# A coupled-oscillator scan: stage values of q moved from SBUF to PSUM, and their squares from VectorE to ScalarE

## The reference

```
i_couple = tanh(q) @ coupling.T
dq = q - q**3 / 3 - p + drive + i_couple + bias
dp = 0.08 * (q + 0.7 - 0.8 * p)
q2 = q + 0.5*DT*dq1;  q3 = q + 0.5*DT*dq2;  q4 = q + DT*dq3
q_next = clip(q + DT/6 * (dq1 + 2*dq2 + 2*dq3 + dq4), -20, 20)     (p likewise)
```

## Time and profile before

| what | value |
|---|---|
| time, median of 3 runs | 1496.73 us (1496.61 to 1496.75) |
| profiled execution, span from its first to its last instruction | 1494.5 us |
| median less that span (what lies around it) | 2.2 us |
| TensorE busy in matmuls, in weight loads | 1429.7 us (96%), 1399.6 us (94%) |
| VectorE busy | 1443.0 us (97%), 11274 instructions |
| ScalarE busy | 724.5 us (48%), 4839 instructions |
| granted clock of TensorE | 0.999 of full speed |
| time that all DMA packets took | 7.6% of 16 engines' span |

### The profile page before, as it was taken

One profiled execution on the slowest core, in us unless ns is written; L12 is line 12 of the kernel. 1 busy time (PEld: TensorE's weight loads), 2 busy tenths in 40 slices (PEclk: granted clock), 3 DMA queues, 4 the chain that ended last, 5 costly groups with the idle time before them and its releaser, 6 DMA issues.

```text
span 1494.5 us, 90834 instructions
## 1 busy us (share of the span) xinstructions
PE 1429.7 (96%) x37025; PEld 1399.6 (94%) x37025; DVE 1443.0 (97%) x11274; ACT 724.5 (48%) x4839; POOL 21.3 (1%) x45
## 2 busy tenths in 40 slices
PE   2578999999999999999999999999999999999998
PEld 0467999999999999999999999999999999999998
DVE  7999999999999999999999999999999999999991
ACT  3344455455455545545554544555455455544541
POOL 0100000000000000000000000000000000000000
PEclk9999999999999999999999999999999999999999
DMA  9200000000000000000000000000000000000000
GB/s 228 46 7 14 8 4 8 21 8 4 25 4 22 7 19 11 4 25 4 22 7 13 16 4 25 4 21 8 11 18 4 25 4 21 8 8 22 4 22 22
DMA packets 11942, 28.41 MB, mean 19 GB/s; under 512 B 1537, under 2 KB 5889, under 8 KB 11393
## 3 DMA queue, kind: packets, MB, share of 16 engines
q1 hardware_dynamic: 11520, 22.57, 6.0%
q10 hardware_dynamic: 2, 0.03, 0.0%
HBM read 18.40 MB, written 4.19 MB: 15 GB/s over the span
## 4 chain that ended last, share of the span: by engine, by line
PE 90%; DVE 6%; ACT 0%; issue 0%; POOLq 0%; DVEq 0%; POOL 0%; ACTq 0%
PE scan_ps L559 52%; PE gu_ps L310 23%; PE y_ps L322 15%; DVE th L631 1%; DVE q_stage L669 1%; DVE with_q L625 1%; DVE q_sq L635 1%; DVE scan_ps L643 1%; DVE q_stage L667 1%; DVE q_cub L638 0%; DVE p_part L625 0%; DVE with_p L625 0%; DVE q_raw L669 0%; DVE q_raw L667 0%; DVE p_state L747 0%; DVE hist L654 0%
## 5 line engine op out<-in xcount | busy, mean ns | idle before, releaser
L559 PE MATMUL scan_ps<-th,wscan 128*128 128x32 f16 (+1 forms) x32768 | 1006.0, 175 | 24.7 <-ACT th L597 24.5
L559 PEld LDWEIGHTS scan_ps<-th,wscan 128*128 128x128 f16 x32768 | 924.5, 96 | 42.1 <-ACT th L597 33.2
L597 ACT ACTIVATE th<-q_stage 128x16 f16<-128x16 f32 x1536 | 318.7, 208 | 524.5 <-DVE q_stage L667 524.5
L310 PE MATMUL gu_ps<-hist,wffn 128*128 128x128 f32 x2816 | 503.8, 285 | 0.0
L310 PEld LDWEIGHTS gu_ps<-hist,wffn 128*128 128x128 f32 x2816 | 394.4, 192 | 0.0
L631 DVE TENSOR_TENSOR th<-t,th 128x16 f16<-128x16 f32 x2048 | 358.1, 175 | 0.3
L322 PE MATMUL y_ps<-wffn,h 128*128 128x128 f32 x1408 | 323.7, 313 | 0.0
L599 ACT ACTIVATE t<-q_stage 128x16 f32<-128x16 f32 x1536 | 306.2, 199 | 0.0
L322 PEld LDWEIGHTS y_ps<-wffn,h 128*128 128x128 f32 x1408 | 209.7, 189 | 0.4 <-DVE h L338 0.4
L597 ACT ACTIVATE th<-q_raw 128x16 f16<-128x16 f32 x512 | 106.3, 208 | 184.7 <-DVE q_raw L667 174.8
L388 ACT ACTIVATE sum_r<-dr,constant 128x64 f32<-128x64 f32 x528 | 174.2, 333 | 16.9 <-DMA dr<-drive 16.9
(11 more groups left out here) (41 smaller groups left out, 562.8 us busy)
## 6 DMA issues: line engine op xcount, KB each, us to landing
raw<-packed SPq DMA_DIRECT2D x11, 768.0 KB, 10.4
dr<-drive SPq DMA_DIRECT2D x34, 128.0 KB, 3.0
xres<-x SPq DMA_DIRECT2D x16, 256.0 KB, 3.6
out<-osb SPq DMA_DIRECT2D x16, 256.0 KB, 3.0
coup<-coupling_t SPq DMA_DIRECT2D x1, 1024.0 KB, 12.5
sc<-scales ACTq DMA_DIRECT2D x1, 33.0 KB
q_raw<-cond_t SPq DMA_DIRECT2D x1, 16.0 KB, 5.5
bias<-bias_t SPq DMA_DIRECT2D x1, 2.0 KB, 6.2
```

The costliest lines, as they stand in the source:

```text
L310: i = nc.tensor.matmul(gu_ps[b][:, half * P:(half + 1) * P], wffn[:, u, j * P:(j + 1) * P], hist[1 - f.parity][:, kt].rearrange("p t b -> ...
L559: i = nc.tensor.matmul(to if both else to[:, 0], wscan[:, w, part, kt, cols], moving if both else moving[:, 0], start=first, stop=last, sk ...
L597: nc.scalar.activation(th[s % 2][:, c, 0, :], q[:, c, :], ACT.Tanh, scale=1.0 / S).then_inc(now.tanh_hi, 1)
```

## The change

q2, q3 and q4 (`q_stage`) no longer lie in SBUF. They lie in PSUM, in the banks in which the local part lies: `scan_ps` grows from 3 banks to 4, the first half of q in the second bank and the second half in the third. The reduces of stages 0 to 2 write there, ScalarE's tanh reads there. `q_raw` (the input of stage 0) stays in SBUF.

In stages 1 to 3 of each step (a step's stages 2 to 4, in the words of the reference) q squared is made by ScalarE, in one instruction of 32 numbers behind the four tanhs, and signalled by a new semaphore `squared`. `cube` waits for it. VectorE's own square is left in stage 0 alone. All of VectorE's instructions that read `q_stage` now stand behind that wait: `cube`, the `with_q2`/`with_q3` rows and the `p_part` sums. The sign of the square changes, and with it two operations.

```diff
-CUBE = [-COEF[STAGE_COEF[i]] / (3 * S * S) for i in range(4)]
+CUBE = [COEF[STAGE_COEF[i]] / (3 * S * S) for i in range(4)]
...
-LOCALS = STEPS * 22
+LOCALS = STEPS * 19
...
+        self.squared = sem("squared")
...
-        q_stage = [sb(f"q_stage{i}", [P, KT, B]) for i in (2, 3, 4)]
...
-        scan_ps = ctx.enter_context(nc.psum_tensor("scan_ps", [P, 6 * APART], F32))
+        scan_ps = ctx.enter_context(nc.psum_tensor("scan_ps", [P, 8 * APART], F32))
...
-            slots = scan_ps[:, half * 3 * APART:(half + 1) * 3 * APART].rearrange("p (k r) -> p k r", k=3)
+            slots = scan_ps[:, half * 5 * APART:(half * 5 + 3) * APART].rearrange("p (k r) -> p k r", k=3)
...
-        local_ps = scan_ps[:, 2 * APART:4 * APART].rearrange("p (h r) -> p h r", h=2)[:, :, 0:HB]
+        middle = scan_ps[:, 2 * APART:8 * APART].rearrange("p (h r) -> p h r", h=2)
+        local_ps = middle[:, :, 0:HB]
+        q_stage = [middle[:, :, (4 + i) * HB:(5 + i) * HB] for i in range(3)]
...
+        def q_half(i, half):
+
+            if i == 0:
+                return q_raw[:, half * HC:(half + 1) * HC, :]
+            return q_stage[i - 1][:, half].rearrange("p (c b) -> p c b", b=B)
...
-                    nc.scalar.activation(t32[:, c, :], q[:, c, :], ACT.Tanh,
+                    nc.scalar.activation(t32[:, c, :], q, ACT.Tanh,
                                          scale=1.0 / S).then_inc(now.tanh_32, 1)
+                if s % 4:
+                    nc.scalar.activation(halves(q_sq[:, :, :]), q_stage[s % 4 - 1], ACT.Square,
+                                         scale=CUBE[s % 4] ** 0.5).then_inc(now.squared, 1)
...
+            def cube(s):
+
+                i = s % 4
+                dve.wait_ge(now.squared, s - s // 4)
+                return local(nc.vector.scalar_tensor_tensor(halves(q_cub[:, :, :]), halves(q_sq[:, :, :]), OWN[i],
+                                                            q_stage[i - 1], ALU.subtract, ALU.mult))
...
+            def add_staged(to, row, column, base):
+
+                q = q_stage[column - BY_Q2]
+                return add(halves(to[:, :, :]), q, float(BY[row, column]), halves(base[:, :, :]))
+
+            def add_p_staged(i):
+
+                return add(halves(p_part[i][:, :, :]), halves(p_part[i - 1][:, :, :]), P_SUM[i], q_stage[i - 1])
...
-                nc.vector.tensor_reduce(q_next[:, 0:HC, :], three[0], AX.X, ALU.add).then_inc(now.q_ready, 1)
+                nc.vector.tensor_reduce(q_half(following, 0), three[0], AX.X, ALU.add).then_inc(now.q_ready, 1)
...
                 s = 4 * t + 1
                 ffn_part(s)
-                dve.wait_ge(now.q_ready, 2 * s)
-                squared = square(1, q2)
                 low_part(s, 0)
-                dve.wait_ge(now.local, squared)
-                cubed = cube(1, q2)
                 low_part(s, 1)
+                add(p_part[0][:, :, :], p_state[:, :, :], P_SUM[0], q1)
+                cubed = cube(s)
+                row3 = add_p(t, 3, 1)
                 dve.wait_ge(now.local, cubed)
                 local_in(s)
-                add(p_part[0][:, :, :], p_state[:, :, :], P_SUM[0], q1)
-                add_q(with_q2[0], 2, BY_Q2, q2, with_q1[1][:, :, :])
-                row3 = add_p(t, 3, 1)
+                add_staged(with_q2[0], 2, BY_Q2, with_q1[1])
                 finish(s)
...
```

More of the change, by code:

```diff
@@ L588, in act_block @@
             for s in range(STAGES):
-                q = q_raw if s % 4 == 0 else q_stage[s % 4 - 1]
                 for half in range(2):
                     c = slice(half * HC, (half + 1) * HC)
+                    q = q_half(s % 4, half)
                     if s:
@@ L596, in act_block @@
                         act.wait_ge(before.q_ready, 2 * STAGES - 1 + half)
[L597 removed]
+                    nc.scalar.activation(th[s % 2][:, c, 0, :], q, ACT.Tanh,
                                          scale=1.0 / S).then_inc(now.tanh_hi, 1)
[L599 removed]
+                    nc.scalar.activation(t32[:, c, :], q, ACT.Tanh,
                                          scale=1.0 / S).then_inc(now.tanh_32, 1)
+                if s % 4:
+                    nc.scalar.activation(halves(q_sq[:, :, :]), q_stage[s % 4 - 1], ACT.Square,
+                                         scale=CUBE[s % 4] ** 0.5).then_inc(now.squared, 1)
                 if s == 1 and before:
@@ L632, in low_part, with square_first, cube_first @@
                                         ALU.subtract).then_inc(now.tanh_lo, 1)
[L634 to L639, removed]
+            def square_first(q):
+                return local(nc.vector.scalar_tensor_tensor(q_sq[:, :, :], q, CUBE[0], q, ALU.mult, ALU.mult))
+            def cube_first(q):
+                return local(nc.vector.scalar_tensor_tensor(q_cub[:, :, :], q_sq[:, :, :], OWN[0], q,
+                                                            ALU.subtract, ALU.mult))
+            def cube(s):
[3 more added lines that the diff above has]
+                                                            q_stage[i - 1], ALU.subtract, ALU.mult))
             def local_in(s):
@@ L643, in local_in @@
                 nc.vector.scalar_tensor_tensor(local_ps, halves(linear[i]), UNIT[i], halves(q_cub[:, :, :]),
-                                               ALU.mult, ALU.add).then_inc(now.first_half, 1)
+                                               ALU.mult, ALU.subtract).then_inc(now.first_half, 1)
             def add_p(step, first, rows):
@@ L663, in finish @@
                 i = s % 4
-                q_next = q_raw if i == 3 else q_stage[i]
+                following = (i + 1) % 4
                 dve.wait_ge(now.first_half, 2 * s + 2)
-                nc.vector.tensor_reduce(q_next[:, 0:HC, :], three[0], AX.X, ALU.add).then_inc(now.q_ready, 1)
+                nc.vector.tensor_reduce(q_half(following, 0), three[0], AX.X, ALU.add).then_inc(now.q_ready, 1)
                 dve.wait_ge(now.second_half, s + 1)
-                nc.vector.tensor_reduce(q_next[:, HC:KT, :], three[1], AX.X, ALU.add).then_inc(now.q_ready, 1)
+                nc.vector.tensor_reduce(q_half(following, 1), three[1], AX.X, ALU.add).then_inc(now.q_ready, 1)
             for t in range(STEPS):
                 q1 = hist[now.parity][:, :, t - 1, :] if t else hist[1 - now.parity][:, :, STEPS - 1, :]
-                q2, q3, q4 = (x[:, :, :] for x in q_stage)
                 s = 4 * t
@@ L693, in dve_block @@
                     dve.wait_ge(before.clipped, STEPS)
-                squared = square(0, q1)
+                squared = square_first(q1)
                 low_part(s, 1)
                 dve.wait_ge(now.local, squared)
-                cubed = cube(0, q1)
+                cubed = cube_first(q1)
                 add_q(with_q1[0], 1, BY_Q1, q1, with_p[:, 1])
@@ L721, in dve_block @@
                 add_q(with_q1[2], 3, BY_Q1, q1, with_p[:, 3])
-                dve.wait_ge(now.q_ready, 2 * s)
-                squared = square(2, q3)
                 low_part(s, 0)
-                dve.wait_ge(now.local, squared)
-                cubed = cube(2, q3)
                 low_part(s, 1)
+                cubed = cube(s)
+                p2 = add_p_staged(1)
                 dve.wait_ge(now.local, cubed)
                 local_in(s)
-                p2 = add(p_part[1][:, :, :], p_part[0][:, :, :], P_SUM[1], q2)
-                with_23 = add_q(with_q2[1], 3, BY_Q2, q2, with_q1[2][:, :, :])
+                with_23 = add_staged(with_q2[1], 3, BY_Q2, with_q1[2])
                 dve.wait_ge(now.local, p2)
-                add(p_part[2][:, :, :], p_part[1][:, :, :], P_SUM[2], q3)
+                add_p_staged(2)
+                dve.wait_ge(now.local, with_23)
+                add_staged(with_q3, 3, BY_Q3, with_q2[1])
                 finish(s)
                 s = 4 * t + 3
[L737 to L740, removed]
                 low_part(s, 0)
-                p4 = add(p_part[3][:, :, :], p_part[2][:, :, :], P_SUM[3], q4)
                 low_part(s, 1)
-                dve.wait_ge(now.local, squared)
-                cubed = cube(3, q4)
+                cubed = cube(s)
+                p4 = add_p_staged(3)
+                dve.wait_ge(now.local, cubed)
+                local_in(s)
                 dve.wait_ge(now.local, p4)
@@ L749, in dve_block @@
                                                        ALU.max, ALU.min))
-                dve.wait_ge(now.local, cubed)
-                local_in(s)
                 if t + 1 == HS:
```

## The result

The changed kernel takes 1539.5 us (1538.8 to 1540.5) against 1496.7 us: a ratio of 1.0288 (95% interval 1.0275 to 1.0301). It is slower by 42.8 us where 39.3 were forecast.

The account below looks back on a forecast made before the run. Bound: the wait ending last in each stage's loop, not busy shares. 240 steps x 0.17 = 41 us, plus 1 for block 0, less 3 for output pieces, gave +39: 1536 us, 2.6% slower; range 1508 to 1613 with 0.80.

Parts of the forecast that it names:

- What bounds the kernel: Each stage is a loop of reduce, tanh, products, reduce; TensorE, VectorE and the local part meet within some 0.03 us.
- Stage by stage: Stages 0 to 3 of a step: 1.37, 1.35, 1.43, 1.43 us, a step 0.17 longer than before.
- The cube's start: VectorE's cube in stages 2 and 3 starts 0.77 us after the first reduce, where it stood at 0.68.
- The square as a close second: ScalarE's square lasts 0.18 us and is there at R + 0.58, just ahead of the cube at R + 0.60.
- The rule of 0.22: A VectorE instruction reading the result of the one just before starts 0.22 us after it; an independent one 0.10 to 0.12.
- VectorE's access to PSUM: Writing q to PSUM makes a reduce 0.22 us and tanh start 0.25 after it; reading q there adds nothing.
- Rival 2: VectorE's reads of q in PSUM cost 0.06 us more each: +0.30 a step beyond the forecast, 1613 us; chance 0.06.
- The sum: Whole kernel: 240 steps x 0.17 = 41 us, block 0 adds 1, output pieces take off 3: +39, 1536 us.
- The term for the output pieces: Stages 1 with an output piece: VectorE's idle time swallows most of it, some 30 at 0.1, 3 us off; least certain.
- TensorE waiting for tanh hundreds of times: Sign that the forecast is right: TensorE's listed waits for tanh rise to hundreds, where there were 65.
- Block 0 and the others about equally long: Sign that the forecast is right: block 0, without FFN, lasts about as long as the blocks with it.
- Rival 1: ScalarE's tanhs gain nothing from PSUM, so the cube waits for the square: +0.63 us a step, 1655 us; chance 0.07.

Follow-up runs that it names:

- the third experiment: Changed kernel with VectorE reordered: first with_p row made at the next step's start, p_part sums and with_q2 row moved forward; 1482.7 us, ratio 0.9901 to the kernel before.
- the fourth experiment: Changed kernel with q_stage back in SBUF, square still on ScalarE and VectorE's order kept; 1631.8 us, ratio 1.0897 to the kernel before.

## Why the prediction was right, point by point

- *What bounds the kernel*: a stage as a loop, with three bounds within 0.03 us. Right: the step grew with the two reduces that came later, and with TensorE back at the bound in the third experiment the step is 5.36, 4 x 1.34.
- *Stage by stage*: 1.37, 1.35, 1.43, 1.43 forecast, 1.36, 1.36, 1.44, 1.43 measured: 0.17 a step was the term, and it held.
- *The cube's start*: 0.77 forecast, 0.79 and 0.78 measured, but by errors that cancel, which was luck. A tanh from PSUM lasts 0.18, not 0.16, and stands 0.06 to 0.08 behind the one before, not 0.06; the second reduce comes 0.15 after the first ahead of stage 2 and, where TensorE no longer holds it, 0.12 ahead of stage 3 (611.80 and 611.92), not 0.17. The groups by shape:

```profile
L605 ACT ACTIVATE th<-scan_ps 128x16 f16<-128x16 f32 x1536 | 266.8, 185 | 558.2 <-DVE scan_ps L694 558.2
L607 ACT ACTIVATE t<-scan_ps 128x16 f32<-128x16 f32 x1536 | 262.2, 182 | 0.0
...
L610 ACT ACTIVATE q_sq<-scan_ps 128x32 f32<-128x32 f32 x768 | 162.8, 212 | 0.0
```

- *The square as a close second*: closer than forecast, a tie. It lasts 212 ns on average, not 180.
- *The rule of 0.22 for an instruction that reads VectorE's own last result*: the two rows that it was read from have an independent one between them (at 594.30). It held: 0.22 with one between (611.48 to 611.70), 0.21 with none (p_state to with_p, 612.91 to 613.12).
- *VectorE's access to PSUM*: the write costs less than was put in, the read nothing. The reduce before, then the reduce and the cube after:

```profile
L667 DVE TENSOR_REDUCE q_stage<-scan_ps 128x16 f32<-128x48 f32 x768 | 158.8, 207 | 4.7 <-PE scan_ps L559 1.0
```

```profile
L694 DVE TENSOR_REDUCE scan_ps<-scan_ps 128x16 f32<-128x48 f32 x768 | 163.2, 213 | 7.6 <-PE scan_ps L567 0.7
...
L656 DVE SCALAR_TENSOR_TENSOR q_cub<-q_sq,scan_ps 128x32 f32<-128x32 f32 x768 | 140.4, 183 | 0.0
```

  The reduce lasts 213 ns, with 207 when it wrote to SBUF and 0.22 us forecast; the cube with q from PSUM 183, as much as its like from SBUF, and its room is 0.10 (611.15 to 611.25), as it was (595.43 to 595.53). Rival 2, with 0.06 more for each read, is out. This is also where the Trainium skill ("Perfetto Trace Analysis", section "Optimizing Scalar/DVE Operations") and this trace differ: 125 ns for VectorE on PSUM against 60 on SBUF would have shown as some 65 ns for each read.
- *The sum*: the main term, 0.17 x 240 = 41 us, held. Block 0 lost 2.4 us, not 1 (87.9 to 90.3 from reduce to reduce): its stages 1 and 2 last 1.40 and 1.45, not 1.35 and 1.43. The term for the output pieces, -3 us, held too: a stage 1 with one went from 1.46 to 1.36, and there are two in a block. What the sum left out goes the other way. After the four stages 1 of a block with a third FFN product the second reduce waits for TensorE (it comes 0.20 after the first, not 0.15), and stage 2 lasts 1.49 instead of 1.44. Where `with_p` waits for `sum_r`, twice a block, stage 3 lasts 1.49, 0.07 over the others, where that wait added 0.04 before. Together that is, over the 15 blocks with the FFN, 15 x (4 x 0.05 + 2 x 0.03) = 4 us. 41 + 2.4 - 3 + 4 is 44, about what the two profiled executions differ by (1538.7 against 1494.5 us); the medians differ by 42.8, since the profiled execution of the changed kernel was its slowest (1540.5).
- *The signs*: "TensorE waiting for tanh hundreds of times" was wrong as a sign. The waiting is there, in stages 3 and 0 as forecast, and only the weight loads show it. "Block 0 and the others about equally long" held: 90.3 us from reduce to reduce in block 0, 90.4 in block 6.
- *Rival 1* (ScalarE gains nothing from PSUM, 1655 us) was worked out for a kernel much like the one of the fourth experiment: 1631.8, with stages of 1.36, 1.46, 1.59 and 1.57 where the rival had 1.37, 1.47, 1.60 and 1.60. In the changed kernel the tanhs last 0.18 and stand 0.06 to 0.08 apart, so it is out.

## What to carry to other kernels

Work that is taken off a busy engine is worth only what it took from the path: here 61 us of VectorE's time went, and the kernel lost 43, since the result came back later, and two waits of VectorE for results of its own stood between it and the reduce, one behind the other. When an input comes later, write anew what stands behind it: put beside its wait what doesn't need it, put two dependent rows two places apart, and move behind the hand-over what the next engine doesn't wait for. Look at a producer's own loads or starts for the waiting of a pipelined engine, not at its busy share.

## What the runs showed of the hardware

- ScalarE's instructions from PSUM take 0.06 to 0.08 of room (612.04 to 612.39 above), but their durations grow when several follow each other so closely: tanh 0.18, 0.18, 0.19, 0.20, the square 0.23, the sum behind it 0.38 (356 ns on average, 333 before). The tanhs' and the square's ends stand 0.07 to 0.10 apart. The FFN's square of 512 numbers, which follows them, went from 577 to 616 ns on average. What limits the ends wasn't tried.
- Two reduces with nothing between them start 0.12 apart when nothing holds the second, with 48 numbers read by each; the one pair in the earlier trace rows stands 0.17 apart.
- ScalarE's room for a tanh of 16 numbers is 0.11 from SBUF and 0.06 to 0.08 from PSUM; VectorE's for 32 numbers is 0.10 from either. In this kernel the gain in moving so small an operand to PSUM is ScalarE's alone.
